# First attention and routing in new queue orders: grouped roots, one choice of experts, six subtractions on VectorE

## The reference

```
x = x + tanh(g0)  * attention0(layernorm(x), ctx)      # one head, softmax over 120 keys, no scale
x = x + tanh(g0f) * experts(layernorm(x))              # 12 experts, the best 2 of each token; 8 real, 4 identity
x = x + tanh(g1)  * attention1(layernorm(x), ctx)      # 16 heads
x = x + tanh(g1f) * linear_fp8(layernorm(x))           # both operands rounded to fp8

logits = einsum('btd,ed->bte', x, gate_w) + expert_bias
topk_logits, topk_idx = top_k(logits, 2); topk_w = softmax(topk_logits)
h = silu(einsum('btd,efd->btef', x, w1)); y = einsum('btef,edf->bted', h, w2)
out = einsum('bte,bted->btd', w_ffn, y) + w_zero[..., None] * x
```

## Time and profile before

| | us |
|---|---|
| three runs | 377.76 (median), 378.01, 376.36 |
| the profiled execution | 376.44, of it span 374.6 |
| PE busy | 343.1 |
| DVE busy | 262.8 |
| ACT busy | 219.1 |
| POOL busy | 159.9 |

### The profile page before, as it was taken

The page is one execution under the profiler, slowest core; times in us unless marked ns, Lnnn a source line. Parts: engine busy times, 40 slices in busy tenths (PEclk is TensorE's granted clock), DMA queues, the critical chain, the costliest instruction groups (busy, mean ns, idle before and its releaser), DMA issues.

```text
span 374.6 us, 9087 instructions
## 1 busy us (share of the span) xinstructions
PE 343.1 (92%) x2977; PEld 275.1 (73%) x2978; DVE 262.8 (70%) x663; ACT 219.1 (58%) x452; POOL 159.9 (43%) x216
## 2 busy tenths in 40 slices
PE   3999989496999999999999998879999999999995
PEld 2688866374999999999999993556667666666674
DVE  2569999985556566545445547879788988867796
ACT  2499997333445544544544542475867787775586
POOL 7189899514365565555556434421130232101100
PEclk9999999699999999999999999999999999999999
DMA  6999931202223333323223214310121000000005
GB/s 192 311 416 417 420 135 75 96 0 72 81 78 124 112 106 118 112 70 80 72 75 81 56 58 138 115 59 2 58 60 41 17 3 0 2 5 2 0 28 198
DMA packets 15386, 38.25 MB, mean 102 GB/s; under 512 B 3574, under 2 KB 4748, under 8 KB 13820
## 3 DMA queue, kind: packets, MB, share of 16 engines
q1 hardware_dynamic: 10556, 26.74, 19.5%
q0 software_dynamic: 3936, 10.45, 9.4%
q10 hardware_dynamic: 864, 0.66, 0.6%
HBM read 24.34 MB, written 13.50 MB: 101 GB/s over the span
## 4 chain that ended last, share of the span: by engine, by line
PE 77%; DVE 11%; ACT 5%; DMA 3%; issue 3%; POOL 0%; ACTq 0%; POOLq 0%
PE two L1985 14%; PE two L1972 14%; PE two L2121 5%; PE two L2004 4%; PE two L2151 4%; PE two L2186 4%; PE two L2107 4%; PE two L2087 3%; PE two L1995 2%; PE two L1850 2%; PE two L2178 2%; PE two L1797 2%; DMA y_d<-y_sb,goal_i 2%; PE two L1777 1%; PE two L1747 1%
## 5 line engine op out<-in xcount | busy, mean ns | idle before, releaser
L1371 DVE SCALAR_TENSOR_TENSOR gate<-th,two 128x512 f32<-128x512 f32 x39 | 26.8, 688 | 58.1 <-ACT th L844 34.4
L844 ACT ACTIVATE th<-two 128x512 f32<-128x512 f32 x39 | 23.3, 598 | 70.4 <-PE two L1985 40.5
L585 POOL DMA_INDIRECT y_d<-y_sb,goal_i x39 | 38.5, 987 | 51.0 <-ACT y_sb L854 51.0
L579 POOL DMA_INDIRECT xg<-xn_d,slot_i x39 | 37.8, 970 | 29.7 <-DVE slot_i L1324 12.2
L1972 PE MATMUL two<-wh,gh 128*128 x156 | 44.2, 283 | 0.2 <-issue 0.2
L1972 PE MATMUL two<-wh,gl 128*128 x156 | 44.0, 282 | 0.0
L1972 PE MATMUL two<-wl,gh 128*128 x156 | 43.8, 281 | 0.0
L599 POOL TENSOR_TENSOR rstd<-var,half 128x2 f32<-128x2 f32 x14 | 9.8, 701 | 77.0 <-DVE var L1438 77.0
L1471 DVE TENSOR_REDUCE nm<-two 128x8 f32<-128x960 f32 x32 | 36.1, 1152 | 4.5 <-PE two L2107 4.1
L536 POOL TENSOR_TENSOR wl<-wl,wh 128x512 fp32r<-128x512 f32 x29 | 36.9, 1293 | 1.7 <-ACT wh L726 1.7
L942 ACT ACTIVATE pT<-two 120x1024 f32<-120x1024 f32 x32 | 31.1, 1038 | 7.0 <-PE two L2121 7.0
(11 more groups left out here) (298 smaller groups left out, 877.3 us busy)
## 6 DMA issues: line engine op xcount, KB each, us to landing
wl<-in_wmoe SPq DMA_DIRECT2D x8, 1024.0 KB, 14.1
y_d<-wh SPq DMA_DIRECT2D x4, 1024.0 KB
yg<-y_d SPq DMA_DIRECT2D x7, 512.0 KB, 3.5
xn_d<-xq SPq DMA_DIRECT2D x8, 256.0 KB, 2.0
xz<-xn_d SPq DMA_DIRECT2D x8, 256.0 KB
out_x<-of SPq DMA_DIRECT2D x8, 256.0 KB, 2.0
x_sb<-in_x SPq DMA_DIRECT2D x1, 1024.0 KB, 9.8
x_sb<-in_x SPq DMA_DIRECT2D x1, 768.0 KB, 4.6
```

The costliest lines, as they stand in the source:

```text
L579: pool.indirect_dma_start(xg[:, n % 2, :], None, xn_d, bass.IndirectOffsetOnAxis(ap=slot_i[:, n:n + 1], axis=0)).then_inc(gathered[n % 2], 16)
L585: pool.indirect_dma_start(y_d, bass.IndirectOffsetOnAxis(ap=goal_i[:, n:n + 1], axis=0), y_sb[:, n % 2, :], None).then_inc(y_stored[n % 2] ...
L844: nc.scalar.activation(th[:], bank[2 + k][:], ACT.Tanh, scale=0.5).then_inc(th_ok, 1)
L1371: dve.scalar_tensor_tensor(gate[:, k, :], th[:], 1.0, bank[2 + k][:], ALU.add, ALU.mult).then_inc(gate_ok, 1)
```

## The change

Five things change; everything behind the routing stays as it is.

1. `root0` and `root1` work on groups of batches, and whoever waits for a root waits for its group. 2. The choice of experts runs once, over all 16 tiles, behind the last logits; `dif` stands behind `pairs`. 3. VectorE subtracts six chunks instead of three. 4. The queues of all four engines get new orders; on ScalarE the rows of batches 5 to 7 are normalised behind the iotas. 5. On TensorE one warm-up product of two goes, six of the products for the second attention and fewer fillers stand behind the ranks, and `whole` moves in front of the last fillers; its input is reduced behind `goal_i`.

```diff
-        EARLY, FAR = TILES - 2 * U, 64 * P
+        FAR = 64 * P
+        ROOTS0, ROOTS1 = ((0, 1), (1, 4), (4, 8)), ((0, 2), (2, 4), (4, 6), (6, 7), (7, 8))
-        VECTOR_LOW = (6, 14, 22)
+        VECTOR_LOW = (6, 10, 14, 18, 22, 26)
-        half = sb("half", [P, U])
+        half = sb("half", [P, B // 2, U])
...
-            def root0(b):
-                pool.wait_ge(var0_ok, b + 1)
-                own.mark(pool.tensor_tensor(rstd0[:, b, :], var0[:, b, :], half[:], ALU.pow))
+            def root0(k):
+                lo, hi = ROOTS0[k]
+                pool.wait_ge(var0_ok, hi)
+                own.mark(pool.tensor_tensor(rstd0[:, lo:hi, :], var0[:, lo:hi, :], half[:, 0:hi - lo, :], ALU.pow))
...
-                act.wait_ge(rstd1_ok, b + 1)
+                act.wait_ge(rstd1_ok, root_of(b, ROOTS1))
...
-            dve.wait_ge(logit_kept, EARLY // U)
-            highest(0, lg, 0, EARLY)
             stats1(7)
-            mark_highest(0, lg, 0, EARLY)
+            low(22)
             logits_of(6)
-            keep_first(0, 0, EARLY)
-            leave(0, EARLY)
-            highest(1, left, 0, EARLY)
+            low(26)
             logits_of(7)
             dve.wait_ge(logit_kept, B)
-            highest(0, lg, EARLY, TILES)
...
+            highest(0, lg)
+            mark_highest(0, lg)
+            keep_first(0)
+            leave()
+            highest(1, left[:])
+            mark_highest(1, left[:])
+            keep_first(1)
+            dve.tensor_tensor(pairs[:, 0:TILES], ...).then_inc(pairs_ok, 1)
             dve.tensor_tensor(dif[:], top[:, 1, :], top[:, 0, :], ALU.subtract).then_inc(dif_ok, 1)
...
-            dve.wait_ge(wf_in, 16)
-            dve.tensor_reduce(red[:, 1:2], wf_sb[:], ...).then_inc(red_ok, 1)
             dve.wait_ge(rank_done, 1)
...
             dve.tensor_tensor(goal_i[:], slot_i[:], second[:], ALU.add).then_inc(goals_kept, 1)
+            dve.wait_ge(wf_in, 16)
+            dve.tensor_reduce(red[:, 1:2], wf_sb[:], ...).then_inc(red_ok, 1)
...
-            warm(2)
+            warm(1)
...
-            busy(bank[3], 4)
+            busy(bank[3], 2)
             products1(3, 4)
-            busy(bank[3], 8)
+            busy(bank[3], 2)
             pe.wait_ge(pairs_ok, 1)
...
             ins.then_inc(rank_done, 1)
-            whole(1, 1, 4)
-            busy(bank[5], 12)
-            for_group = (4, 6, 7, 9, 10)
+            products1(4, 10)
+            busy(bank[5], 4)
             for n in range(4):
-                products1(*for_group[n:n + 2])
                 pe.wait_ge(onerow_ok, n + 1)
...
             e0, e1 = experts(0), experts(1)
+            whole(1, 1, 4)
             busy(bank[5], 3)
```

More of the change, by code:

```diff
@@ L758, in _ @@
                 high(j)
             spread_std(4)
-            high(8)
-            copy_xT(5)
             high(9)
+            copy_probT(1)
+            for j in range(10, 12):
+                high(j)
+            exp0_of(2)
+            for j in range(12, 14):
+                high(j)
             copy_probT(2)
+            high(14)
+            exp0_of(3)
             copy_xT(6)
-            exp0_of(3)
-            high(10)
+            high(15)
+            spread_std(5)
+            high(16)
@@ L794, in _ @@
                 high(j)
-            copy_xT1(4)
+            copy_probT(5)
+            exp0_of(7)
+            for j in range(24, 26):
+                high(j)
+            copy_xT1(3)
+            high(26)
+            copy_probT(6)
+            for j in range(27, 29):
+                high(j)
+            copy_xT1(4)
+            norm1(1)
+            norm1(2)
+            copy_probT(7)
+            high(29)
+            copy_xT1(5)
             norm1(3)
-            copy_probT(7)
-            high(24)
@@ L799, in _ @@
-            copy_xT1(5)
+            high(30)
+            copy_xT1(6)
             norm1(4)
-            high(25)
-            copy_xT1(6)
             copy_xT1(7)
-            for j in range(26, 28):
-                high(j)
-            norm1(5)
-            for j in range(28, 31):
-                high(j)
-            norm1(6)
-            norm1(7)
             high(31)
@@ L1198, in keep_first, with highest @@
[L1198 to L1205 removed]
+            def highest(k, src):
+                then(dve.tensor_reduce(top[:, k], src, AX, ALU.max))
@@ new lines, in mark_highest, with keep_first, leave @@
+            def mark_highest(k, src):
+                then(dve.tensor_tensor(eq[:], src, wide(top[:, k], E_ALL), ALU.is_equal))
+                then(dve.scalar_tensor_tensor(cand[:], eq[:], -64.0, over(count[:, 0:E_ALL], TILES), ALU.mult, ALU.add))
+            def keep_first(k):
+                then(dve.tensor_reduce(pick[:], cand[:], AX, ALU.min))
+                then(dve.tensor_tensor(hot[:, k], cand[:], wide(pick[:], E_ALL), ALU.is_equal))
+            def leave():
+                then(dve.scalar_tensor_tensor(left[:], hot[:, 0], -3.0e38, lg, ALU.mult, ALU.add))
```

286 lines of the change are left out of this document (126 added, 160 removed).

## The result

Twenty executions of the changed kernel: 371.48 to 380.97 us, median 376.88; twenty of the kernel before: median 377.82, all but one between 375.83 and 378.35. The ratio of the times is 0.988 (95% interval 0.986 to 0.990); it leaves out executions more than 1.5% above a kernel's fastest. Neither the median nor the ratio tells the story, for the new kernel's executions fall into three separate groups: nine at 371.5 to 372.2 (mean granted clock 0.991 to 0.998), five at 376.8 to 377.5 (0.979 to 0.993) and six at 380.2 to 381.0 (0.964). The kernel before has two: six at 375.8 to 376.7 and thirteen at 377.1 to 378.4. Good against good, the new kernel is 4.4 us faster; its six are over 4 us slower than the good ones of before. The mean of all its executions is 375.8, against 377.4, so that 1.5 us is what it gives on the average.

What follows compares the result with a forecast made beforehand. Before the experts no engine alone was the bound but the order in which four queues meet; logits -2.2, choice -3.6, rank -0.4, slots -1.3, `whole` +0.2 gave -7.3: 369.1 on the profile's scale, forecast 369.8 us, range 366 to 375.

Steps and rivals of the forecast that it cites:

- Logits -2.2: End of the first attention: last logits ready at 62.0 instead of 64.20, bounds 59.8 and 70.0.
- Rival 4: Into the experts: choice shorter, but a new wait keeps gather or experts from beginning earlier; 376.4 us, chance 0.07.
- Head: Kernel start: one warm-up product less lets keys start at 12.45 instead of 13.56; gain 1.1 us, bounds 0 and 1.6.
- Choice: Behind the last logits: twelve instructions over all tiles take 4.7 us, GpSimd being nearly finished; term -3.6 us.
- Rank and slots: Behind the choice: shorter TensorE pause gives -0.4 us; slot products following VectorE at once give -1.3 us.
- Roots in groups: GpSimd in the attention: eight of sixteen operation pairs saved at 0.9 us each, 6.4 us lighter behind 19.75.
- Held VectorE products: VectorE in the attention: 1.9 us held in negmax, 0.35 for each of six subtractions; 4.0 us added.
- three floors: Attention work sums without idle time: VectorE 55.4, GpSimd 55.9, ScalarE 56.3 us, within 1 us of each other.
- the walk: New queues timed by hand-overs through the attention, without VectorE's holding: last logits at 59.8, GpSimd's last subtraction at 60.2.
- Rival 2: TensorE's clock or ScalarE's queue takes part back; two clock falls at 1.9 us each give 372.9 us, chance 0.17.
- Rival 3: VectorE and GpSimd hold each other in the attention, 15.1 us over the walk; logits at 70.0, 380.7 us, chance 0.08.
- Rival 1: Attention as walked, nothing more held: last logits at 59.8, 366.9 us on the profile's scale, chance 0.14.

Runs made afterwards that it cites:

- fill_attn: Changed kernel plus ten unread 256-column products in TensorE's pauses of the first attention; median 371.67 us, ratio to before 0.986.
- two_warm: fill_attn with both warm-up products instead of one; median 372.79 us, ratio to the kernel before 0.990.
- route_only: Kernel before with only the single choice for all tiles and the new order behind it; median 374.18 us, ratio to before 0.993.
- tail_before: Changed kernel with the former order of products, fillers, `whole` and its reduction behind the choice; median 376.66 us, ratio to before 0.999.
- single_roots: fill_attn with the roots again one batch at a time; median 375.61 us, good 373.8 to 375.7, ratio to before 0.999.
- max_psum: fill_attn with the row maximum kept in PSUM, so negmax has one SBUF input instead of two; median 371.50 us, ratio to before 0.988.
- after_again: Changed kernel, unmodified, run on another occasion; median 373.02 us, ratio to before 0.986; its profile is of the execution of 373.85.
- three_lows: fill_attn with chunks 10, 18 and 26 subtracted on GpSimd again, three on VectorE; median 372.13 us, ratio to before 0.988.

## Why the prediction was right and where it failed

The sign was right and the good executions (371.5 to 372.2) lie in the range of 366 to 375, 2 us above the 369.8; the median of 376.88 lies outside it. Two things made that: the term "Logits -2.2", mis-sized so far that the logits came later and not earlier, and a rival priced as a sum of falls where it was one long fall.

By the time of each hand-over, counted from the span's start, in fill_attn against before (forecast in brackets): last logits +0.75 (-2.2), choice -3.47 (-3.6), rank -0.46 (-0.4), slots -1.49 (-1.3), `whole` +0.07 (+0.2); in all -4.60 (-7.3), the first expert product at 83.35 against 87.95 in the earlier trace rows. Behind it nothing changed (0.2 us). The four terms behind the logits were forecast at -5.1 together and measured -5.35: that part of the good time is no luck. Rival 4 is out by it.

*Head.* 1.1 was forecast for one warm-up product; two_warm measured 0.9 to 1.1. That the products may then stay slow for 8 us more, at 3.2 us, was not thought of.

*Choice.* Right, and for the reason given: it is short because GpSimd has at most one chunk left. route_only shows it from the other side: the same instructions beside a busy GpSimd took 10.1 us, within the bounds of 4.4 and 15.2.

*Rank and slots.* Right in size. tail_before gave the 1.5 back, and 1.5 more in front of the ranks, of the fillers and a fallen clock together, that no step had.

*Roots in groups.* Mis-sized. The forecast took 0.9 for each grouped power with its product, by the one row of 2 numbers; the powers are 1.01, 1.46 and 1.64. Seven groups behind the head cost 9.3 us (7.9 powers, 1.4 products) instead of 6.3, and 26 subtractions are 2.7 us lighter than 29, not 3.8, since each is longer (1337 ns against 1293). GpSimd, forecast 10.2 us lighter, is 6.7 us lighter. Still worth their place, by single_roots. That is why GpSimd ended the chain in fill_attn from 51.72 on.

*Held VectorE products.* The step that was furthest off: of the 2.95 us by which the logits came later than the 62.0 of the forecast, 1.4 went when its larger half was taken away (max_psum). "I keep the 1.9" for negmax and "0.35 for each" of the subtractions made 4.0. Measured: negmax 6.0 - 8 x 0.16 = 4.7, subtractions 5.7 to 6.0 - 6 x 0.68 = 1.6 to 1.9: some 6.5. The subtractions' share was right; negmax was carried over as if the neighbours would stay, and in the new order seven of eight meet GpSimd in a run of subtractions. max_psum took all 4.7 away and the logits moved by 1.4 only, for other engines were close behind: there the chain of waits from 36 to 63 us runs almost wholly through TensorE, its fillers in it. The forecast had three floors within 1 us of each other (55.4, 55.9, 56.3), and all were too low. VectorE was busy for 46.8 us from 12.25 to 64.95, not 43.0, since its sum held only the 2.1 us of holding of the kernel before. GpSimd's was short by the 3.5 us above. ScalarE's last rounded chunk, 58.5 in the walk, ended at 63.3: its idle time was not filled. TensorE had no floor at all.

*Rival 2* is what happened in at least six of the twenty executions. The mechanism was named, but by the earlier trace rows it was priced at 1.9 us a fall, the time after which the clock was back. In the attention it can be back as soon, some 3 us in after_again; but in the profile of 380.15 it stayed at 0.50 for 23.6 us. In that time the other three engines stood idle for 8 to 10 us each and the chain ran through TensorE. That cost 8.5 us on the path to pairs (last logits 73.40, against 64.95). "Against: a pause of 1.17 us did no harm" was one pause with long products around it. The forecast's own sign of error, a clock of 0.5 between 28 and 60, is what the profile shows.

*Rival 3*, the slower side, did not happen as such; its 0.94 for each negmax was 0.59 on the average and its 1.26 for each subtraction 0.3, so that the sum stayed at 6.5 of its 15.1. *Rival 1* did not happen: more was held than the forecast had, not less.

What stays open: why the clock falls in some executions only, of the same instructions, and for how long. Behind the same five pauses it fell for 23.6 us (the changed kernel), for some 3 us (after_again) and not at all before 62 us (tail_before). The fillers show that the pauses take part in it; what else decides, no run shows. Open too are the five executions of the changed kernel at 376.8 to 377.5 and fill_attn's one at 377.4, of which there is no profile. A late head and a short fall make 5 us in three_lows, the nearest kernel with such a profile (376.88); that it is the same in the others is not shown.

## What to carry to other kernels

When an order is tightened so that three engines are equally loaded, ask first what TensorE does between its products: behind a row of pauses of 0.5 to 1.3 us the clock fell in some executions, for up to 8.5 us, and with unread products in them no execution of 54 had the long fall. The median went down by 1.4 us or by 5, by the occasion that one compares with. Compare groups of executions, not medians, when a clock can fall; a mean granted clock beside each time sorts most of them, though not the late heads, in which the granted clock is recorded as 1.00. A VectorE product on two small SBUF tiles beside a busy GpSimd took 0.54 to 1.13 us seven times of eight here, instead of 0.16; leaving one operand in PSUM took that away, but look at which engine is next before counting the gain.

## What was not expected of the hardware

- The same program gives 371.5 or 380.2: the clock's fall, once begun in a stretch of small products, held for 23.6 us with TensorE busy 94% of it, and in another execution, at the same place and behind the same pauses, for some 3 us.
- GpSimd's power grows with the numbers per partition: 0.69 us for 2, 1.01 for 4, 1.46 for 6, 1.64 for 8.
- At the start products run at about half speed, 1.95 against 1.05 us for the same two, until about 10 us in some executions and until about 18 in others, while the granted clock is recorded as 1.00.
